# Moving the value-table transposes of a fused attention and feed-forward kernel to another place in the sync engine's queue

## The reference, cut to what matters

```
x   = x + attention(layernorm(x), ctx)          # 1600 tokens of 512 channels, 5776 keys, 16 heads of 32
  q = (x @ Wq + bq) * scale;  k, v = split(ctx @ Wkv + bkv)
  q, k = rounded to 255 levels per row and head;  v = rounded to 255 levels per column, over all keys
  a = softmax(q k^T), rounded to 0..255 per row
  x += (a v) @ Wp + bp
x   = x + ffn(layernorm(x))                      # 1408 hidden channels, rounded inputs, relu^2 gate, rmsnorm
```

## Time and profile before

| | |
|---|---|
| time, median of three runs | 1827.62 us |
| the profiled execution, its span | 1827.62 us, 1825.7 us |
| VectorE busy over the span | 1689.5 us (93%) |
| TensorE matmul busy | 1629.9 us (89%) |
| ScalarE busy | 1390.6 us (76%) |
| GpSimd busy | 1375.8 us (75%) |

### The profile page before, as it was taken

One profiled execution on the slowest core, in us unless ns is written; L12 is line 12 of the kernel. 1 busy time (PEld: TensorE's weight loads), 2 busy tenths in 40 slices (PEclk: granted clock), 3 DMA queues, 4 the chain that ended last, 5 costly groups with the idle time before them and its releaser, 6 DMA issues.

```text
span 1825.7 us, 41871 instructions
## 1 busy us (share of the span) xinstructions
PE 1629.9 (89%) x17054; PEld 1151.7 (63%) x17054; DVE 1689.5 (93%) x2670; ACT 1390.6 (76%) x1364; POOL 1375.8 (75%) x759
## 2 busy tenths in 40 slices
PE   9997999989898889888898898888898888789998
PEld 7884666666566666655666666555555555478776
DVE  7869999999999999999999999999999999976764
ACT  3447889888998898889898898898888888743222
POOL 2443798899889888988898889888898898742322
PEclk9998999999999999999999999999999999899999
DMA  6678988998999989889999998889998997832221
GB/s 204 208 210 211 204 184 183 188 194 164 187 185 199 192 181 191 177 167 185 197 198 181 186 190 173 163 159 181 183 166 171 202 189 147 198 76 62 51 59 48
DMA packets 851675, 309.97 MB, mean 170 GB/s; under 512 B 784982, under 2 KB 814236, under 8 KB 851356
## 3 DMA queue, kind: packets, MB, share of 16 engines
q1 hardware_dynamic: 850476, 306.96, 81.9%
q10 hardware_dynamic: 1008, 0.33, 0.1%
HBM read 74.26 MB, written 39.59 MB: 62 GB/s over the span
## 4 chain that ended last, share of the span: by engine, by line
DVE 69%; PE 20%; issue 6%; DMA 3%; POOL 1%; ACT 1%; SPq 1%; POOLq 0%; DVEq 0%; ACTq 0%
DVE S L1307 63%; PE PS L884 5%; PE PK L921 3%; PE PS L751 2%; PE PK L685 2%; PE PK L683 2%; PE PS L716 2%; DVE MJ L1333 1%; DVE kam L1200 1%; DVE VMX L1204 1%; PE PO L685 1%; PE PO L683 1%; DMA XIT<-XI 1%; DMA PP<-Pr 1%; PE PO L770 1%
## 5 line engine op out<-in xcount | busy, mean ns | idle before, releaser
L1307 DVE TENSOR_SCALAR_CACHE_REDUCE S<-PS,SQN 128x1536 f32<-128x1536 f32 (+1 forms) x768 | 1281.9, 1712 | 7.8 <-PE PS L751 6.9
L1541 POOL CAST PT<-PP 128x3072 uint16<-128x3072 uint8 (+1 forms) x400 | 1047.6, 2648 | 207.3 <-DMA PP<-Pr 201.8
L1103 ACT ACTIVATE Pr<-S,MS 128x5888 uint8<-128x5888 f32 x200 | 1041.2, 5206 | 162.5 <-DVE MJ L1333 151.1
L751 PE MATMUL PS<-KT,QT 96*128 96x512 bf16 (+1 forms) x2496 | 631.0, 372 | 162.7 <-DVE S L1307 145.6
L770 PEld LDWEIGHTS PO<-VI,PT 128*128 128x128 f16 x9200 | 338.3, 96 | 178.9 <-issue 24.1
L751 PEld LDWEIGHTS PS<-KT,QT 96*128 96x128 bf16 (+1 forms) x2496 | 189.1, 98 | 378.1 <-DVE S L1307 137.2
L770 PE MATMUL PO<-VI,PT 128*128 128x32 bf16 x9200 | 355.8, 177 | 3.7 <-ACT AO L1052 3.2
L685 PE MATMUL PK<-CT,WG 128*128 128x128 f32 (+1 forms) x1288 | 210.0, 290 | 1.8 <-DMA WG<-Wkv 1.8
L683 PE MATMUL PK<-WG,CT 128*128 128x128 f32 (+1 forms) x1288 | 208.9, 291 | 0.8 <-ACT VV L957 0.4
L685 PEld LDWEIGHTS PK<-CT,WG 128*128 128x128 f32 x1288 | 166.5, 191 | 4.8 <-issue 2.7
L683 PEld LDWEIGHTS PK<-WG,CT 128*128 128x128 f32 (+1 forms) x1288 | 165.6, 190 | 3.4 <-issue 1.1
(11 more groups left out here) (161 smaller groups left out, 1555.2 us busy)
## 6 DMA issues: line engine op xcount, KB each, us to landing
CT<-ctxt SPq DMA_DIRECT2D x180, 256.0 KB, 3.3
k_rows<-KS SPq DMA_DIRECT2D x39, 512.0 KB, 4.0
q_rows<-QS SPq DMA_DIRECT2D x13, 512.0 KB, 4.7
W13F<-w13T SPq DMA_DIRECT2D x12, 352.0 KB, 3.6
PP<-Pr SPq DMA_TRANSPOSE x200, 6.0
XT<-x SPq DMA_DIRECT2D x12, 256.0 KB, 4.6
XR<-x SPq DMA_DIRECT2D x12, 256.0 KB, 3.4
base_rows<-XO SPq DMA_DIRECT2D x12, 256.0 KB, 3.4
```

The lines of the kernel that those rows point to most:

```text
L751: last = pe.matmul(PS[n % 2][p0:p0 + r, f:f + w], QT[h % 3][0:PARTS * HD, q0:q0 + r], KT[h % 3][0:PARTS * HD, c * CHUNK + f:c * CHUNK + f ...
L1103: act.activation(Pr[i % 2].rearrange("p t q b -> p t b q"), S[i % 2].rearrange("p (t b q) -> p t b q", b=2, q=P), ACT.Exp, bias=MS[:, i % ...
L1307: v.tensor_scalar(S[i % 2][:, c * CHUNK:c * CHUNK + CW[c]], PS[n % 2][:, 0:CW[c]], neg_step, None, ALU.mult, ALU.min, accum_out=MN[:, i % ...
L1541: gp.tensor_copy(PT[i % 2][:, 2 * t0:2 * t1, :].rearrange("p (t b) q -> p t b q", b=2), PP[i % 2][:, t0:t1, :].bitcast(U8).rearrange("p t ...
```

## The change

Three edits.

1. In `plan_transfers` the load of a turn of `VI` is counted one step earlier and at half its size, and the loads of `WP` are no longer counted.
2. In SyncE's block of a step, `turn_v` moves from before the head pieces to behind the wait for the exponential, directly ahead of the wait for the widening and the transpose of `Pr`.
3. In GpSimd's due times, `b * 2 // 3` becomes `b * 2 / 3` for `v_quant`.

```diff
         for b in range(NBT):
             load[batch_step(g, b) + K_STORE] += len(BATCH[b]) * P
-            load[STEP_OF_UNIT[g, NU - 1] + 6 + b * 2 // 3] += 2 * P
-    for k in range(NK):
-        load[WP_AT + k] += P * C // 256
+            load[STEP_OF_UNIT[g, NU - 1] + 5 + b * 2 // 3] += P
...
                 for k, first in EARLY_W.items():
                     if 0 <= i - first < WSP:
                         load_w13(k, i - first)
-                for g, b in v_turns.get(i, []):
-                    turn_v(g, b)
                 for h, piece in sorted(HEAD_PIECES.get(i, []), key=lambda w: w[1]):
                     load_head(h, piece)
...
                     sp.dma_start(halves(k)[2], w13T[k * P:(k + 1) * P, :]).then_inc(M["f_w1"], 16)
+                for g, b in v_turns.get(i, []):
+                    turn_v(g, b)
                 if i >= 2:
                     sp.wait_ge(M["s_un"], NCAST * (i - 1))
...
-                             (end + 5.95 + b * 2 // 3, v_quant, (g, b))]
+                             (end + 5.95 + b * 2 / 3, v_quant, (g, b))]
```

## The result

The changed kernel takes 1845.49 us as the median of four runs (1842.71 to 1847.09), against 1827.43 us for the kernel before beside it: a ratio of 1.0096, 95% interval 1.0076 to 1.0115. Forecast were 4.1 us, with a range that ended at 1836.5 us. The profiled execution took 1849.93 us.

The account below looks back on a forecast made before the run. VectorE was taken to set the pace. Crowded steps 0.7 + 0.7 + 1.3, other even steps 0.4, one-sided error 0.6, less 0.2, made 3.5; TensorE's 0.6 made 4.1: 1827.6 + 4.1 = 1831.7 us, range 1828.0 to 1836.5.

Parts of the forecast that it names:

- The 9.7 us of room: Step 50: SyncE's delay plus landing may take 9.7 us from the exponential's end before VectorE waits; 3.7 us late at median landing.
- Step 156: Third group: three head pieces in step 152 start its transpose some 4 us later, costing VectorE 0.4 us at step 156.
- the signs named: New profile: later transposes in steps 44 to 50, and longer waits of ScalarE for landings, VectorE for ScalarE, TensorE for `PT`.
- the working of step 50: Step 50: `QT`, `KT` and a pair of turns start the transpose of `Pr` 3.4 us later; VectorE waits 0.7 us at 54.
- With 0.5 us for what the steps before it are later by now: Step 50: earlier steps make SyncE 0.5 us later, so it is free at 528.0 us instead of 527.46.
- The 0.15 us a place: Four crowded places: 0.15 us added for each because longer landings add in full; 0.6 us together.
- The forecast wait was 0.9 us: Step 154: the transpose of step 150 starts about 2.9 us later and costs VectorE 0.9 us.
- The other even steps: Nine even steps before each group's last: turns behind the wait cost 0.05 us each, 0.4 us together.
- The room is enough: First rival: step 50's transpose goes out under 3.7 us behind the exponential, only 0.5 us of waits stays: 1828.1 us; chance 0.16.
- TensorE too: Second rival: late `PT` holds up `values` and the scores behind it, 5 us beside the 3.5: 1836 us; chance 0.12.
- The first rival's "6.6 us": Step 50: claimed against that rival that the four issues can't be done in less than 6.6 us plus the transpose before.
- Faster: Third rival: moving the turns frees head pieces and transposes they held up, 0.5 us gained: 1827.1 us; chance 0.05.

Follow-up runs that it names:

- the `KT` put back: Edit 1 alone, with the first `KT` of heads 5, 9 and 13 back in steps 52, 102 and 152, against the kernel before: 1832.42 us, ratio 1.0026.
- the two split kernels: Whole change with only the last three, or only the first nine, turn batches behind the wait, against the kernel before: 1837.96 us (1.0064) and 1848.48 us (1.0116).
- the probes: Two kernels: the kernel before plus unused transposes, alone or in rows, in steps without turns and head pieces; 1828.74 and 1828.79 us.
- the first probe: The kernel before plus unused transposes: one, two and three of `KT` size in steps 62, 70, 78, four of turn size in 84; 1828.74 us.

## Why the prediction was wrong

**The bound and the chain were right.** VectorE sets the pace, and the loss goes from SyncE over the landing and ScalarE to VectorE, about one us for one once the last moment for the exponential, 539.5 us in the times of before, is passed. The 9.7 us of room, counted from the end of step 50's exponential, did not hold: that exponential had itself waited for a landing and ended 1.2 us later against VectorE than before (538.51 - 7.48 = 531.03 against 529.80), which leaves 8.5 us. Also right were the direction and the steps 54, 104 and 154. Step 156 lost nothing in the changed kernel itself; the traces show a loss there only with edits 1 and 2 together (2.1 us) and with the `KT` put back. Edit 3 was taken at 0, and alone it measured 0, with an interval of about 2.7 us to either side. Of the signs named, the transposes of the steps 44 to 48 went out 3.4 to 3.5 us late (at least 2.5 was forecast), that of step 50 6.4 us late (4.4), and ScalarE's wait for landings rose to 28.0 us (20 or more); VectorE's wait for ScalarE rose to 11.1 us where some 3 was forecast.

**The step that failed is the working of step 50**, which gave 0.7 us. To lay it beside the trace, 7.48 us are taken off the times after, by which VectorE is behind there; its end of step 53 is then at 544.94, as before (544.90).

| | forecast | measured, less 7.48 |
|---|---|---|
| SyncE free of step 49's transpose | 528.0 | 529.6 |
| from there to the transpose of step 50 | 6.2 | 7.8 |
| its landing | 6.0 | 6.4 |
| VectorE waits at step 54 | 0.7 | 4.3 |

The three differences are 1.6, 1.6 and 0.4 us, together 3.6, and 0.7 + 3.6 is the 4.3 measured. Three things went wrong in this step of the working, and one more was left out.

- *"With 0.5 us for what the steps before it are later by now"* failed first. A turn behind the wait makes the block of an even step as long as the step, so a delay that enters at step 44 isn't worked off until step 50: the transposes go out 3.4 to 3.5 us behind their exponentials in 44, 46 and 48, and SyncE, free for step 45 2.2 us later than before, was still 2.1 us late for step 50. The transpose of step 49 came 2.4 us later than before, shorter by 0.25 in its own issue. That is what the two split kernels show: 1.4 to 1.6 us of loss at step 54 with the first turns in the old place, 4.3 to 5.1 behind the wait.
- The issues at their single durations failed second. The pair took 3.64 us instead of 2.5, `KT` 1.86 instead of 1.47. With edit 1 alone `QT` and `KT` took 5.2 instead of 3.0, and the probes show the same without a turn near.
- The landing was a small error at step 50, but with edit 1 at step 100 it was 7.6 us, 1.6 us in full. The 0.15 us a place for it was too little.
- A term was missing: that a stall stops TensorE and lowers its granted clock afterwards. It is 0.3 us at step 54 and 1.6 us at step 154, some 2 us in all, and makes a long stall cost more than itself. The matmuls at the lower clock show it; no run held the clock up for comparison.

Step 154 fails in the same terms. SyncE's issues of step 150, before:

```profile
1246.80 2.59 SPq L446 DMA_TRANSPOSE VI<-VB  x2
1249.48 4.08 SPq L627 DMA_TRANSPOSE PP<-Pr  x1
```

and after, with the landing of the last one:

```profile
1264.29 1.52 SPq L465 DMA_TRANSPOSE QT<-q_rows  x1
1265.85 1.81 SPq L475 DMA_TRANSPOSE KT<-k_rows  x1
1267.76 2.94 SPq L444 DMA_TRANSPOSE VI<-VB  x2
1270.74 3.59 SPq L625 DMA_TRANSPOSE PP<-Pr  x1
```

```profile
DMA to landing us min/median/max: 7.3/7.3/7.3
```

Less the 16.5 us by which VectorE is behind there, the transpose goes out 4.7 us later than before where 2.9 was forecast, 1.0 us of it since SyncE came late; and it lands after 7.3 us instead of 6.0. The forecast wait was 0.9 us; with 1.8 and 1.3 more, less the 0.9 that VectorE had by then waited at step 152, it is 3.1, and 3.17 was measured. The 1.62 us behind it come on top.

The crowded steps, for which the sum took 2.7 + 0.6 us, cost 4.8 + 2.8 + 5.1 = 12.7 us. The range was built round these terms, with bounds of 0 to 4 us on the largest, and so stopped at 1836.5.

**The other even steps** were taken at 0.4 us. The place of the turns alone costs 5.4 us in its trace and 0.2% in its runs. In the trace 3.1 us are at step 152, where the first probe lost 1.9 us without this edit, and 1.2 us over the steps 49 to 54.

**The rivals.** "The room is enough" decided by 3.7 us of delay; it was 6.4. The Trainium skill's rule behind it ("DMA: Bandwidth & Descriptors", section "Issuing engines are not separate DMA queues") speaks of an issue that is small beside the DMA; the trace doesn't agree, since the issues of step 50 ahead of the transpose of `Pr` took 7.8 us and its landing 6.4. "TensorE too" was the nearest in time, at 1836 us still 9 us short, and not in its mechanism: TensorE's wait for `PT` rose from 5.2 to 21.1 us, longest 5.8, but VectorE waits for TensorE's scores only 2.1 us more, and 1.9 us of its waits for them stand behind a stall, at the lower clock. With edit 2 alone TensorE's wait for `PT` is as large, 21.4 us in 24 pieces, and that kernel lost only 0.2%. That a late `PT` costs something of its own was not shown. The first rival's "6.6 us" for the four issues of step 50 is a slip: their terms in the same text (0.6, 1.53, 1.47, 2.5) make 6.1. "Faster" has nothing for it.

**What stays open.** Why an issue is longer in a row, whether by bytes under way or by the number of transfers in the queues, was not told apart; nor why one behind a store takes 3.3 us. Whether the edits add up is not decided: 0.46, 0.20 and -0.01% make 0.65%, by their intervals some 0.4 to 0.9%, and the whole measured 0.96% (0.76 to 1.15). Whether edit 3 costs something beside edit 2 is open too (1.0054 against 1.0020, with intervals that just touch, and nothing of it in the trace). No version here beats the kernel before; there VectorE waits for ScalarE 0.2 us in all, so the place of these transposes has next to nothing to give.

## What to carry to other kernels

A queue's list is to be costed as a chain from the first step that changes, with what each step hands on to the next: here the turns behind the wait cost about 1 us by themselves at step 54, and took away what the crowded step needed. Issues in a row are costed above the median of single ones: five of them, in step 50, took 7.8 us where 6.2 was reckoned. The landing behind them came after 5.4 to 7.6 us in the crowded steps 50, 100 and 150, so such a stall is forecast as a range of 2 us, and not as one number. A planner that moves work forward by a step or two can put it where the queue has no time, so its new list is to be read at the steps that were full before.

## What was not expected of the hardware

- The issue of a transpose on SyncE has no fixed length: 1.35 to 1.39 us for one of 1536 columns alone, 1.9 us each for two or three in a row, 3.3 us for one right behind a store of keys that itself takes 0.39 us.
- After 4.4 us with little to do TensorE's granted clock was 0.50 for 5.6 us; with edit 1 alone, around a gap of 6.4 us without a matmul, it fell to 0.50 in the gap and stayed there for 4.5 us behind it. The kernel before goes to 0.50 too without such a stall, among other places for 6.8 us from 437.6, 799.4 and 1157.8 us, where TensorE had been busy for 4.8 to 5.8 of the 6.4 to 6.8 us ahead. VectorE is busy for 93 to 98% of these stretches, so the lower clock by itself need not cost it much.
- The same list gave stalls of 2.8 and 5.2 us at one step in two executions, with landings of 5.43 and 7.04 us for the same transpose, while the medians of the two sets of runs agreed within 0.1% (1845.49 and 1844.77 us).
- The part up to the end of step 0, which is the same program in all, differed by up to 8.2 us between profiled executions (-1.7 to +6.4 against before), with one load of 7.13 us for 5.07 in the longest. A difference of some us between two profiles says nothing until this part is taken off.
